# Row tiles of a segment sum: one load for each tile into a ring of 64, or one load for each slot from two queues

## The reference

```python
alpha = s_i[row] + s_j[col] + b_att           # row = src, col = dst
alpha = jnp.where(alpha >= 0, alpha, 0.2 * alpha)
alpha = jnp.exp(alpha - amax[row])
alpha = alpha / (asum[row] + 1e-16)
msg = alpha[:, :, None] * xh[row]             # 100,000 messages of 4 x 32
out = jax.ops.segment_sum(msg, col, num_segments=n)
deg = jax.ops.segment_sum(jnp.ones(...), col, num_segments=n)
```

## Time and profile before

| | us |
|---|---|
| runs of the kernel before, median (lowest to highest) | 6873.23 (6869.83 to 6882.63) |
| the profiled execution's own time | 6882.63 |
| its span in the trace | 6880.9 |
| stretch of the phase `l0m`, from its first load to the end of its last addition | 445.4 |
| POOL busy over the whole span | 4232.0 (62%) |
| DVE busy over the whole span | 4509.8 (66%) |

### The profile page before, as it was taken

The page is one execution under the profiler, slowest core; times in us unless marked ns, Lnnn a source line. Parts: engine busy times, 40 slices in busy tenths (PEclk is TensorE's granted clock), DMA queues, the critical chain, the costliest instruction groups (busy, mean ns, idle before and its releaser), DMA issues. The chain is left out here.

```text
span 6880.9 us, 125007 instructions
## 1 busy us (share of the span) xinstructions
PE 4477.9 (65%) x25221; PEld 3485.8 (51%) x25222; DVE 4509.8 (66%) x14383; ACT 2634.4 (38%) x7366; POOL 4232.0 (62%) x4983
## 2 busy tenths in 40 slices
PE   5777777503555554664666666766666665988986
PEld 4566656403444443553555554335555554666665
DVE  8777777543444444667544446867777776877777
ACT  2355555302333333666000002833333334544443
POOL 0077777726777775334777774037777771777774
PEclk9988888755555555887665566978888886888888
DMA  1144444467111112551333331022233321333332
GB/s 64 33 144 150 144 146 148 112 50 56 54 54 53 53 53 78 126 127 43 79 79 79 79 79 42 0 54 75 74 74 74 76 68 37 75 73 73 73 73 53
DMA packets 833938, 528.65 MB, mean 77 GB/s; under 512 B 588596, under 2 KB 741000, under 8 KB 833416
## 3 DMA queue, kind: packets, MB, share of 16 engines
q1 hardware_dynamic: 702152, 261.57, 17.4%
q0 software_dynamic: 131648, 265.56, 13.7%
HBM read 399.11 MB, written 127.68 MB: 77 GB/s over the span
## 5 line engine op out<-in xcount | busy, mean ns | idle before, releaser
L1362 POOL DMA_INDIRECT l2e_rows<-l_rows,k_src_of x832 | 840.8, 1011 | 600.0 <-POOLq L224 346.7
L1362 POOL DMA_INDIRECT spare<-l_rows,k_dst_of x784 | 749.4, 956 | 385.6 <-issue 237.2
L826 POOL DMA_INDIRECT src_records<-sort_rec,sort_idx x784 | 785.2, 1001 | 309.3 <-issue 233.1
L1227 POOL DMA_INDIRECT dst_rows<-l0d_out,l0d_idx x832 | 800.1, 962 | 271.3 <-issue 215.1
L1362 POOL DMA_INDIRECT table<-l_rows,k_dst_of x784 | 741.4, 946 | 296.2 <-issue 238.6
L2227 PE MATMUL l2e_pV<-l2e_rows,ident 128*128 128x512 f32 x416 | 291.5, 789 | 356.4 <-DMA l2e_rows<-l_rows,k_src_of 356.0
L1186 PE MATMUL l0d_pX<-table,l0d_ohT 128*128 x1664 | 460.5, 457 | 95.8 <-issue 52.6
L1186 PEld LDWEIGHTS l0d_pX<-table,l0d_ohT 128*128 128x128 f32 x1664 | 392.5, 326 | 149.1 <-issue 149.1
L2251 ACT ACTIVATE table<-l2e_pV 128x128 f32<-128x128 f32 x832 | 219.1, 278 | 555.1 <-PE l2e_pV L2232 555.1
L1600 DVE TENSOR_TENSOR l1e_prod<-l1e_pG,table 128x512 f32 (+1 forms) x196 | 135.5, 691 | 450.1 <-DMA table<-l_rows,k_dst_of 412.2
L1345 PE MATMUL l0m_pR<-l0m_rows,spare 128*128 x1664 | 298.4, 337 | 196.8 <-DVE both L1313 125.8
(11 more groups left out here) (418 smaller groups left out, 13188.4 us busy)
## 6 DMA issues: line engine op xcount, KB each, us to landing
l0m_rows<-dst_rows SPq DMA_DIRECT2D x196, 264.0 KB, 2.8
sort_rows<-lo_rows SPq DMA_DIRECT2D x196, 256.0 KB
sort_rec<-rec SPq DMA_DIRECT2D x98, 472.0 KB
l2e_lrow<-dst_local SPq DMA_DIRECT2D x208, 128.0 KB
table<-src_records SPq DMA_DIRECT2D x196, 128.0 KB
table<-src_records SPq DMA_DIRECT2D x196, 100.0 KB
dst_rows<-l0d_out,l0d_idx POOLq DMA_INDIRECT x832
l2e_rows<-l_rows,k_src_of POOLq DMA_INDIRECT x832
```

The source lines that it names most:

```text
L826: e.indirect_dma_start(kn.by_src_rec[:, :], bass.IndirectOffsetOnAxis(ap=r["idx"][:, st.quad, j:j + 1], axis=0), r["rec"][:, st.quad, j, : ...
L1227: e.indirect_dma_start(kn.by_dst[:, :], bass.IndirectOffsetOnAxis(ap=r["idx"][:, st.quad, j:j + 1], axis=0), r["out"][:, st.quad, j, :], N ...
L1362: e.indirect_dma_start(r["rows"][:, i % ring, j, 0:width], None, table[:, :], bass.IndirectOffsetOnAxis(ap=columns[:, i * G + j:i * G + j ...
```

## The change

The phase `l0m` loads a tile for each slot. For each step SP issues two transfers of one tile (slots 2 and 3) and POOL two (slots 0 and 1), each addressed by a register that is loaded from `slot_reg`. The ring holds 8 steps of four tiles. POOL subtracts only the block's first node, for two steps at once (`local`), and DVE copies the two other fields, for two steps at once (`keep`). DVE makes one one-hot matrix in each step, ACT three. `trio` and the operations that clear and fill it at the end of `l0d` go. Places of small tensors change too: `kn.cut` has memory of its own, `kn.first` as well, and `kn.gate` lies in `kn.first`.

The diff, cut to the parts that work:

```diff
@@ l0_messages, end of the vector engine's part
             ch(e.memset(kn.both[:, :], 0.0))
-            ch(e.memset(kn.trio[:, :, :], 0.0))
-            ch.wait()
-            ch(e.tensor_copy(kn.trio[:, :, 1], kn.local[:, 0, :]))
             ch.wait()
@@ l0_sums
+    def loaded(e, r, pair):
+        for st in pair:
+            e.wait_ge(r[f"ld{st.ring}"], st.eighth * 32 + 32)
+            e.wait_ge(r[f"ld_first{st.ring}"], st.eighth * 32 + 32)
...
         def sync(e, ch):
             def load(st):
-                wait_step(e, r["summed"], st, 4)
-                wait_step(e, r["taken"], st, 4)
-                e.dma_start(r["rows"][:, bass.ds((st.i % KEEP) * (G * DROW), G * DROW)].rearrange("p (t c) -> p t c", c=DROW),
-                            by_tile[:, bass.ds(st.i * G, G), :]).then_inc(r[f"ld{st.quad}"], 16)
-            run_steps(e, ch, [(load, 0)], TSTEPS, QUAD)
+                tiles = slot_values(kn, e, kn.slot_regs["sync"], st, 0)
+                wait_step(e, r["summed"], st, RING)
+                wait_step(e, r["kept"], st, RING)
+                for j in range(2, G):
+                    e.dma_start(r["rows"][:, st.ring, j, :], kn.by_dst[bass.ds(tiles[j] * P, P), :]
+                                ).then_inc(r[f"ld{st.ring}"], 16)
+            run_steps(e, ch, [(load, 0)], STEPS, RING)
         def gpsimd(e, ch):
-            def take(st):
-                at = kept(kn, e, "gpsimd", st)
-                ...
-                for j in range(G):
-                    out = kn.trio[:, bass.ds(st.i * G + j, 1), :].rearrange("p s c -> p (s c)")
-                    ins = e.tensor_tensor(out, r["rows"][:, bass.ds(at[j] * DROW + AW, 3)], out, ALU.subtract)
-                ...
-            run_steps(e, ch, [(take, 1, 1, STEPS)], TSTEPS, QUAD)
-            ... three copies out of kn.trio
+            def load(st):
+                tiles = slot_values(kn, e, kn.slot_regs["gpsimd"], st, 0)
+                wait_step(e, r["summed"], st, RING)
+                wait_step(e, r["kept"], st, RING)
+                take_waits(e, kn.tally)
+                for j in range(2):
+                    e.dma_start(r["rows"][:, st.ring, j, :], kn.by_dst[bass.ds(tiles[j] * P, P), :]
+                                ).then_inc(r[f"ld_first{st.ring}"], 16)
+            def local(pair):
+                both, slots, rows = loaded(e, r, pair)
+                at = both(kn.local[:, 0, slots])
+                e.tensor_tensor(at, rows[:, :, :, AW + 1], at, ALU.subtract).then_inc(r["local"], 2)
+            run_steps(e, ch, [(local, 3, 2), (load, 0)], STEPS, RING)
         def vector(e, ch):
             def hot(st):
-                wait_step(e, r["taken"], st)
+                wait_step(e, r["local"], st)
                 wait_step(e, r["summed"], st, 2)
-                for j in (0, 3)[:1 + st.par]:
-                    ...
+                e.tensor_scalar(r["oh"][:, st.par, 0, :], kn.iota[:, :], kn.local[:, 0, bass.ds(st.i * G, 1)], None,
+                                ALU.is_equal).then_inc(r["hot"], 1)
+            def keep(pair):
+                both, slots, rows = loaded(e, r, pair)
+                ch(e.tensor_copy(both(kn.wt[:, slots]), rows[:, :, :, AW]))
+                e.tensor_copy(both(kn.src_of[:, slots]), rows[:, :, :, AW + 2]).then_inc(r["kept"], 2)
-            run_steps(e, ch, [(hot, 2, 1, STEPS), (add, 4, 1, STEPS)], TSTEPS, RING)
+            run_steps(e, ch, [(hot, 5), (add, 7), (keep, 4, 2)], STEPS, RING)
         def scalar(e, ch):
-                last = 4 - st.par
-                for j in range(1, last):
+                for j in range(1, G):
...
-               sbufs=[("rows", [P, KEEP * G * DROW], F32)],
+               sbufs=[("rows", [P, RING, G, DROW], F32), ("oh", [P, 2, G, P], F32)],
```

More of the change, by code:

```diff
@@ L258, in setup @@
     kn.low_st = nc.alloc_semaphore("low_st")
-    kn.cut = sb("k_cut", [P, SLOTS])
-    kn.first = kn.cut[:, 0:8 * NB].rearrange("p (b k) -> p b k", k=8)
+    kn.first = sb("first", [P, NB, 8])
     kn.first_at = sb("first_at", [P, NB], I32)
@@ L269, in node_buffers @@
     kn.wt = sb("k_wt", [P, SLOTS])
+    kn.cut = sb("k_cut", [P, SLOTS])
     kn.both = sb("both", [P, 2 * NB * AW])
@@ L275, in node_buffers @@
     kn.MT = sb("spare", [P, NB, H])
-    kn.gate = sb("gate", [P, NB])
+    kn.gate = kn.first[:, :, :].rearrange("p b k -> p (b k)")[:, 0:NB]
 def flat(kn, t):
@@ L1054, in l0_messages @@
     kn.sq = flat(kn, kn.MT)[:, 0:3 * SLOTS].rearrange("p (s c) -> p s c", c=3)
-    kn.trio = flat(kn, kn.MT)[:, 3 * SLOTS:6 * SLOTS].rearrange("p (s c) -> p s c", c=3)
     small = kn.tab0[:, :].rearrange("p (b w) -> p b w", w=TW)[:, :, H:TW]
@@ L1243, in l0_sums @@
 def l0_sums(kn):
-    spare = flat(kn, kn.MT)[:, 6 * SLOTS:]
-    by_tile = kn.by_dst[0:EP, :].rearrange("(t p) c -> p t c", p=P)
     def sums(r, st, j):
         return r["pR"][:, st.par, j // 2, (j % 2) * 256:(j % 2) * 256 + AW]
[L1251 to L1257, removed]
+    def loaded(e, r, pair):
+        for st in pair:
+            e.wait_ge(r[f"ld{st.ring}"], st.eighth * 32 + 32)
+            e.wait_ge(r[f"ld_first{st.ring}"], st.eighth * 32 + 32)
+        ring = pair[0].ring
+        return (lambda t: t.rearrange("p (s j) -> p s j", j=G)), bass.ds(pair[0].i * G, 2 * G), r["rows"][:, ring:ring + 2, :, :]
@@ L1326, in hot @@
             def hot(st):
-                wait_step(e, r["taken"], st)
+                wait_step(e, r["local"], st)
                 wait_step(e, r["summed"], st, 2)
-                last = 4 - st.par
-                for j in range(1, last):
-                    ch(e.activation(r["oh"][:, st.par, j, :], kn.iota[:, :], ACT.Abs, bias=place(st, j), scale=-1.0))
+                for j in range(1, G):
+                    ch(e.activation(r["oh"][:, st.par, j, :], kn.iota[:, :], ACT.Abs,
+                                    bias=kn.local[:, 0, bass.ds(st.i * G + j, 1)], scale=-1.0))
                 ch.wait()
-                e.activation(r["oh"][:, st.par, 1:last, :], r["oh"][:, st.par, 1:last, :], ACT.Relu, bias=kn.ones[:, 0:1],
-                             scale=-1.0).then_inc(r["hot_rest"], 1)
-            run_steps(e, ch, [(hot, 2, 1, STEPS)], TSTEPS, QUAD)
+                e.activation(r["oh"][:, st.par, 1:, :], r["oh"][:, st.par, 1:, :], ACT.Relu, bias=kn.ones[:, 0:1],
+                             scale=-1.0).then_inc(r["hot3"], 1)
+            run_steps(e, ch, [(hot, 5)], STEPS, QUAD)
             ch.wait()
```

27 lines of the change are left out of this document (7 added, 20 removed).

## The result

The changed kernel takes 6906.64 us, the median of six runs (6901.86 to 6911.69). The kernel before takes 6869.96 us beside it (six runs, 6863.74 to 6882.63). The ratio is 1.0055 [1.0045, 1.0065], so the change makes the kernel slower, by 37 us. The forecast was 6942, with a range of 6825 to 7030.

A forecast was written before the change was run, and what follows sets the result against it. The prediction took waits around the ring of four to bound l0m before, and POOL's transfers after: 208 x 2.42 = 504 us plus 11 for head and drain, 515 against 445.4, +69, so 6942 us in medians, range 6825 to 7030.

The forecast's parts named there:

- The likeliest case: In l0m, POOL's transfers bound at d from 1.0 to 1.3 us: slower by 7 to 137 us, chance 0.62.
- The ring of four: Loads in l0m wait for PE four steps back, 8.5 us a turn; eight places take this wait off the path.
- POOL's queue is the next bound: In l0m, four transfers and one subtraction on POOL take 4.85 us for two steps, 2.42 a step.
- The price d of a plain transfer: On POOL in l0m, start to start: between 0.45 and 1.26 us, taken as 1.15, near its indirect transfer.
- The register load: On POOL in l0m: 0.48 us, put at nothing, as hidden under the making of the previous transfer.
- The 11 us for head and drain: At l0m's ends: first landing, then last load's landing, subtraction, ACT, PE and DVE work, added to 504 us.
- The floor by landing: POOL's subtraction in l0m waits for loads: two steps last at least d + L + 0.25, 4.2 to 4.95 us.
- The cheap transfer, the faster rival: POOL's plain transfer under 0.9 us, compute or landing bounds l0m: 396 us, 49 less, kernel 6824; chance 0.25.
- The rival in which nothing is hidden: POOL's register load serial and transfers at indirect price: 3.1 us a step, l0m 656 us, +210; chance 0.08.
- SP: SP's two transfers and register work in l0m take 1.4 us a step, off the path; splitting queues buys nothing.
- Compute at 1.85: ACT, DVE and PE work in l0m would allow some 1.85 us a step.
- DVE keeping POOL from writing descriptors: VectorE's two-port mode might block POOL's descriptors in l0m, 60 us in all; no sign seen, no term given.

The follow-up runs named there:

- e7: Kernel before the change with a ring of three steps in place of four: l0m 588.3 us against 445.3, ratio to the kernel before 1.0186.
- e8: Changed kernel with three transfers of a step on POOL and one on SP: l0m 590.0 us, ratio to the kernel before 1.0193.
- e3: Changed kernel with POOL's subtraction one step later in its queue: l0m 452.6 us against 480.2, ratio to the kernel before 1.0017.
- e4: Changed kernel with POOL's register load placed ahead of the subtraction: l0m 455.4 us against 480.2, ratio to the kernel before 1.0028.
- e6: Changed kernel with the edits of e3 and e4 together: l0m 452.5 us against 480.2, ratio to the kernel before 1.0021.
- e10: e6 with the two copies of keep on ACT in place of DVE: l0m 452.0 us, ratio to the kernel before 1.0020.
- e1: Changed kernel with one transfer of a step on POOL and three on SP: l0m 478.2 us against 480.2, ratio to the kernel before 1.0055.
- e2: Changed kernel with all four transfers of a step on SP, POOL only subtracting: l0m 591.2 us, ratio to the kernel before 1.0183.
- e12: The kernel before the change, unedited, traced again beside e9 to e11: l0m 441.3 us against 445.3 first profiled.
- e9: e6 with POOL reading its four tile numbers for two steps in one register load: l0m 472.5 us, ratio to the kernel before 1.0045.
- e11: e6 with the edits of e9 and e10 together: l0m 472.8 us, ratio to the kernel before 1.0036.

## Why the prediction was right, and which of its terms were mis-sized

Direction and range came true, the path through POOL did as well, but the sum was right in part by luck. The likeliest case, slower, was given for a price of a transfer from 1.0 to 1.3 us. Measured was 0.61, the condition of the rival that made the kernel faster. It came out slower because two terms that the sum had at nothing, the register load and the gap in the chain through the landing, put back what the price took away.

**The ring of four.** Right, and shown by e7. With eight places it is off the path (SP still waits for PE, but ahead of POOL), and another bound stands in its place.

**POOL's queue is the next bound.** Right: e8 pays for an added transfer in full, e3 and e4 gain by moving what stands in that queue, and in e3, e6 and e10 the queue runs without a wait. In the changed kernel it is not alone: the wait for the landing lies in it and adds some 27 us. But one sign named for it was wrong: POOL was to be busy for over 80% of the stretch, and is for 51%. A queue can be full with the engine half idle, since register loads and conversions aren't busy time.

**The price d of a plain transfer.** Mis-sized. I took 1.15, near POOL's indirect transfer; it is 0.61 from start to start (0.54 busy). That lies between the bounds of 0.45 and 1.26, but on the other side: nearest to SP's. That the indirect transfer reads a list of row numbers may be why it costs twice as much; no run shows the cause. This alone takes 4 x 0.54 = 2.16 us from the 4.85 of two steps.

**The register load.** Mis-sized: put at nothing, hidden under the previous transfer, and it isn't hidden. It and what goes with it (in the second gap the subtraction's handing over and a part of the wait for the landing) leave gaps of 0.76 and 1.12 us in two steps where back-to-back transfers leave 0.06: 1.76 us more. With 0.1 ahead of the subtraction this brings the sum back to 4.6. Two errors of opposite sign thus nearly cancelled: 2.42 a step forecast, 2.30 measured, +69 us forecast and +37 measured. A closer sum might have been had from the rows at hand: the 0.30 of idle ahead of every indirect transfer, where nothing is waited for, was in the prediction as the mark of unhidden sequencer work, and was argued away. The 11 us for head and drain are a small error: the parts named for them add up to 10, and 485.9 - 207 x 2.304 = 9 were measured.

**The floor by landing.** d + L + 0.25 lacked a term, the gap behind the subtraction before the next transfer can start. With the measured parts it is 0.61 + 2.6 + 0.21 + 1.12 = 4.5 us for two steps, a little over the 4.21 that the full queue takes in e3. That is why e3, which only takes the landing off the path, gains 27.6 us and no more. L itself, read from POOL's gathers as 2.8 to 3.55, is 2.6.

**The cheap transfer, the faster rival.** Its condition held, d being under 0.9, and its result of 396 us for the phase didn't come. It took the register load for hidden, and its floor lacked the gap; with d at 0.61 queue and landing together are what holds the step at 2.3 and not at 1.85. A price under the threshold thus wasn't enough to make the rival come true.

**The rival in which nothing is hidden.** Half of its condition held: the register load is serial. The other half, an indirect transfer's price, didn't, and its +210 us stayed away.

**SP.** 1.4 us a step forecast, 1.67 by the distances of e1. It didn't matter in the changed kernel, but e1 shows it to be near. The prediction also had the split over two queues buy nothing, with SP far from full; with all four transfers on SP (e2) a step takes 2.81 us in place of 2.28. Issuing is what bounds here, and it is the time of issuing that a second queue saves. The issue time in the profile, 0.33, isn't the distance at which SP can issue, 0.525. The prediction had the distance as 0.45, from issue time and register operation added up.

**Compute at 1.85.** Not shown. No version ran below 2.13 a step, and those at 2.13 (e3, e6, e10) are held by POOL's queue: 4.21 us for two steps, 4.29 with the long gaps, which is 2.14. How fast compute alone would go behind this ring stays open. That the kernel before lies at 2.10 to 2.12 is another bound of nearly the same length; e7 shows that it is the ring.

**DVE keeping POOL from writing descriptors.** No sign of it, as weighed. POOL's 416 transfers lie between 534 and 592 ns, with the comparisons and the copies of `keep` running beside them.

**Other phases.** As long as before within the spread of single traces, as forecast: from the end of `l0m` to the end of the program 3732.9 us, against 3747.0 in the first profile of before, which was its slowest run, 3744.9 in e12, and 3745 to 3755 in e9 to e11.

## What to carry to other kernels

Before work moves onto an engine's queue, add up what the sequencer does between its instructions, register loads above all: they are paid in line there, and busy time doesn't show them. A full queue may show as an engine busy for half of the time, with small waits put down to issue. Moving one stage by a step, or adding one instruction, tells whether it is the bound; so do the distances between its instructions, when they repeat to a hundredth of a microsecond while other engines' work changes. When a deeper ring takes one wait away, the gain is bounded by the next chain through the new queue, and that includes the gap ahead of the next transfer, not only the landing.

## What the hardware showed that I had not expected

- A plain transfer of 128 rows costs POOL 0.54 us (534 to 592 ns, 416 of them), an indirect one of 128 rows 0.94 to 0.97 (321 gathers of layer 2).
- SP issues plain transfers of one tile 0.525 us apart at best, while each shows as 0.33 us; over a register load 1.15.
- A register load of four numbers takes 0.32 us on POOL where they lie beside each other, and 0.975 where they are read as two pairs with a stride.
- The gap of POOL behind its subtraction is 1.06 to 1.12 us in the changed kernel's rows, with a register load in it, and 0.52 in e4's, without.
- With two plain transfers a step in its queue, POOL stands idle for 2.50 us between two of them, once in 100 (behind the transfers 113, 213, 313 and 413 of `l0m` in the changed kernel, e3, e6 and e10 alike). With three a step (e8) it is 2.3 us, once in 93.
- A wait in POOL's queue can hide under the transfer before it: the profile gives 10.5 us of waiting for loads, and taking that wait away gained 27.6.
